# Value projections of 20 of the 64 attention units made ahead, during the gates and mixing stages

## What is computed

```python
q = query @ W_Query + B_Query          # query: normalized x after layer 0
k = key @ W_Key + B_Key                # key = value = the context
v = value @ W_Value + B_Value
scores = jnp.einsum('bqhd,bkhd->bhqk', q, k) / D ** 0.5
probs = jax.nn.softmax(scores, axis=-1)
out = jnp.einsum('bhqk,bkhd->bqhd', probs, v)
```

## Time and profile before

| | |
|---|---|
| median of 3 runs | 1844.22 us (1844.12 to 1845.14) |
| span of the profiled execution | 1843.2 us |
| busy: PE, PEld, DVE, ACT, POOL | 1663.1, 1128.1, 1209.8, 843.8, 608.1 us |
| gates stage | about 4 to 64 us of the span |
| mix and MLP | about 64 to 437 us, of it steps -2 and -1 to 126.5 us |
| attention | about 437 to 1650 us |
| one attention unit | 18.17 us |

### The profile page before, as it was taken

One profiled execution on the slowest core, in us unless ns is written; L12 is line 12 of the kernel. 1 busy time (PEld: TensorE's weight loads), 2 busy tenths in 40 slices (PEclk: granted clock), 3 DMA queues, 4 the chain that ended last, 5 costly groups with the idle time before them and its releaser, 6 DMA issues. The chain is left out here.

```text
span 1843.2 us, 25796 instructions
## 1 busy us (share of the span) xinstructions
PE 1663.1 (90%) x8789; PEld 1128.1 (61%) x8789; DVE 1209.8 (66%) x2689; ACT 843.8 (46%) x1870; POOL 608.1 (33%) x730
## 2 busy tenths in 40 slices
PE   6569999996999999999999999999999999973584
PEld 4447777754666666666666666666666766642352
DVE  6445656532777777776776776776777677757761
ACT  3324343431555555555555555555555555531110
POOL 2143445430333323332332332333232323220375
PEclk9669999997999999999999999999999999985697
DMA  8100000003323232323232322222223223213254
GB/s 254 27 23 12 12 12 1 1 0 106 69 47 69 47 92 46 69 69 69 47 92 47 67 72 61 54 65 74 56 60 79 59 53 86 46 45 99 44 85 58
DMA packets 68961, 109.46 MB, mean 59 GB/s; under 512 B 18400, under 2 KB 50400, under 8 KB 68832
## 3 DMA queue, kind: packets, MB, share of 16 engines
q1 hardware_dynamic: 62688, 99.29, 22.1%
q0 software_dynamic: 6144, 8.52, 3.0%
HBM read 27.84 MB, written 12.85 MB: 22 GB/s over the span
## 5 line engine op out<-in xcount | busy, mean ns | idle before, releaser
L1128 POOL TENSOR_SCALAR at_Pr<-at_Pr,at_rinv 128x512 f32<-128x512 f32 x512 | 355.8, 695 | 841.2 <-DVE at_rinv L1158 841.2
L1093 ACT ACTIVATE at_Pr<-at_ps,at_nmax 128x512 f32<-128x512 f32 x512 | 352.2, 688 | 535.2 <-DVE at_nmax L1153 533.6
L1153 DVE TENSOR_REDUCE at_nmax<-at_ps 128x1 f32<-128x512 f32 x512 | 351.2, 686 | 154.0 <-PE at_ps L958 142.5
L958 PE MATMUL at_ps<-at_k,at_q 128*128 128x512 f32 x1024 | 420.7, 492 | 10.8 <-DMA at_k<-at_k_own 9.1
L969 PE MATMUL at_ps<-k_ident,at_Pr 128*128 128x128 f32 x2048 | 309.8, 274 | 4.5 <-POOL at_Pr L1128 4.5
L969 PEld LDWEIGHTS at_ps<-k_ident,at_Pr 128*128 128x128 f32 x2048 | 250.5, 140 | 90.2 <-POOL at_Pr L1128 27.7
L1165 DVE COPY at_PT<-at_ps 128x512 f32<-128x512 f32 x384 | 261.4, 681 | 0.0
L958 PEld LDWEIGHTS at_ps<-at_k,at_q 128*128 128x128 f32 x1024 | 174.6, 191 | 130.7 <-issue 121.2
L979 PE MATMUL at_ps<-at_PT,at_V 128*64 128x512 f32 x1024 | 235.4, 602 | 0.9 <-DVE at_PT L1165 0.9
L1158 DVE RECIPROCAL at_rinv<-at_rsum 128x1 f32<-128x1 f32 x512 | 83.3, 163 | 161.1 <-ACT at_Pr L1093 159.1
L979 PEld LDWEIGHTS at_ps<-at_PT,at_V 128*64 128x64 f32 x1024 | 68.1, 137 | 122.5 <-issue 121.4
(11 more groups left out here) (236 smaller groups left out, 1996.5 us busy)
## 6 DMA issues: line engine op xcount, KB each, us to landing
at_k<-at_k_own SPq DMA_DIRECT2D x256, 256.0 KB, 4.3
k_x<-in_x SPq DMA_DIRECT2D x8, 512.0 KB, 8.5
mg_ctx<-in_ctx SPq DMA_DIRECT2D x8, 512.0 KB, 8.7
mx_ctxn<-in_ctx SPq DMA_DIRECT2D x8, 512.0 KB, 3.8
rows<-m_ctxT SPq DMA_DIRECT2D x16, 256.0 KB, 2.6
out<-k_x SPq DMA_DIRECT2D x8, 512.0 KB, 3.5
r_w<-in_L_ffn_w SPq DMA_DIRECT2D x16, 256.0 KB, 5.5
mx_w<-in_L_ffn_w SPq DMA_DIRECT2D x2, 1024.0 KB, 10.0
```

The costliest lines, as they stand in the source:

```text
L958: ins = pe.matmul(ps[:, S_BANK + j % 2, :], q2[:, u % 2, h, q:q + P], k2[:, u % 2, h, part, :], start=part == 0, stop=part == 1)
L1093: act.activation(Pr[:, j % 4, :], ps[:, S_BANK + j % 2, :], ACT.Exp, bias=nmax[:, j % 4:j % 4 + 1], accum_out=rsum[:, j % 4:j % 4 + 1]).th ...
L1128: pool.tensor_scalar(Pr[:, n % 4, :], Pr[:, n % 4, :], rinv[:, n % 4:n % 4 + 1], 1.0, ALU.mult, ALU.mult).then_inc(s["pn"], 1)
L1153: dve.tensor_reduce(nmax[:, j % 4:j % 4 + 1], ps[:, S_BANK + j % 2, :], AX.X, ALU.max, negate=True).then_inc(s["nmax"], 1)
```

## The change

20 of the 64 value projections (units 0 to 19) are made earlier, into two spare PSUM banks, copied by ACT into four slots of the tile `hT` (idle until step 0), written to a DRAM tensor of 20 x 256 KB by SP, and in the attention stage loaded back, one DMA per unit. The work is cut in halves of a unit (8 passes of 128 columns). 8 halves go behind the last gate map, 2 behind the first small transposes, 9 into step -2 and 21 into step -1 of the mixing, at the points named in `EARLY_HALVES`. W_Value is loaded for it into the other half of `hT`, and to make room the context's buffer in the gates stage shrinks from 8 batches to 3, so that SP waits for transposes before it loads further. `pick_half` is made in the gates stage, ahead of its wait for the gate maps.

In the attention loop the units whose successor has its values ready (u = 0 to 18) have no value projection; the key projection stands in block 0, and the query projection in block 4, where the values were. ACT takes the queries out in block 5 and DVE makes their second parts in block 5.

```diff
+EARLY_V = 20
+V_SLOTS = 4
+EARLY_HALVES = {"gates": 8, "rows": 2, (-2, "scores"): 1, (-2, "keys"): 2, (-2, "values"): 3, (-2, "states"): 3,
+                (-1, "scores"): 1, (-1, "keys"): 7, (-1, "values"): 9, (-1, "states"): 3, (-1, "turned"): 1}
+EARLY_AT = dict(zip(EARLY_HALVES, itertools.accumulate(EARLY_HALVES.values(), initial=0)))
...
+def early_values_pe(pe, fl, ctxT_all, ps, banks, point):
+
+    at = EARLY_AT[point]
+    for n, half in (divmod(h, 2) for h in range(at, at + EARLY_HALVES[point])):
+        b, hp = n // HP, n % HP
+        if half == 0 and n >= 2:
+            pe.wait_ge(fl["out"], n - 1)
+        if n == 0 and half == 0:
+            pe.wait_ge(fl["w"], 16)
+        for t in (2 * half, 2 * half + 1):
+            for d in range(DC):
+                ins = pe.matmul(ps[:, banks[n % 2], P * t:P * t + P],
+                                ctxT_all[:, d, b * S + P * t:b * S + P * t + P], fl["wv"][:, d, P * hp:P * hp + P],
+                                start=d == 0, stop=d == DC - 1)
+        if half:
+            ins.then_inc(fl["ps"], 1)
+
+
+def early_units(point):
+
+    at = EARLY_AT[point]
+    return range(at // 2, (at + EARLY_HALVES[point]) // 2)
+
+
+def early_values_act(act, fl, ps, banks, point):
+
+    for n in early_units(point):
+        act.wait_ge(fl["ps"], n + 1)
+        if n >= V_SLOTS:
+            act.wait_ge(fl[f"put{n % V_SLOTS}"], 16 * (n // V_SLOTS))
+        act.copy(fl["stage"][:, n % V_SLOTS, :], ps[:, banks[n % 2], :]).then_inc(fl["out"], 1)
+
+
+def early_values_sp(sp, fl, point):
+
+    for n in early_units(point):
+        sp.wait_ge(fl["out"], n + 1)
+        sp.dma_start(fl["dram"][n], fl["stage"][:, n % V_SLOTS, :]).then_inc(fl[f"put{n % V_SLOTS}"], 16)
...
-                    sp.dma_start(ctx_s[:, i, :, :], cv[i]).then_inc(s[f"c{i % RING}"], 16)
+                    if i >= CTX_RING:
+                        sp.wait_ge(s["ctx_turned"], i - CTX_RING + 1)
+                    sp.dma_start(ctx_s[:, i % CTX_RING, :, :], cv[i]).then_inc(s[f"c{i % RING}"], 16)
...
+                load_wv(sp)
...
+                early_values_sp(sp, fl, "gates")
+                early_values_sp(sp, fl, "rows")
...
                 gate_maps(B // 2 - 1)
+                early_values_pe(pe, fl, ctxT_all, ps, V_BANKS, "gates")
 
                 pe.wait_ge(s["rows"], 4)
                 for t in range(TPB):
                     at = R * (KIND_G + t)
                     pe.transpose(ps[:, COL_BANK, at:at + R], gg[:, P * t:P * t + P], ident[0:R, 0:R])
+                early_values_pe(pe, fl, ctxT_all, ps, V_BANKS, "rows")
...
                 act.activation(lfg[:, :], efg[:, :], ACT.Ln, bias=1.0).then_inc(s["act_rows"], 1)
+                early_values_act(act, fl, ps, V_BANKS, "gates")
                 act.wait_ge(s["rows"], 6)
...
                 act.activation(floor[:, :], logmax[:, :], ACT.Exp, scale=-1.0).then_inc(s["act_rows"], 3)
+                early_values_act(act, fl, ps, V_BANKS, "rows")
...
+                for k in range(2):
+                    at = slice(R * k, R * k + R)
+                    dve.tensor_copy(g["pick_half"][at, :, :], ident[at, at].rearrange("k (r a) -> k r a", a=1
+                                                                                   ).broadcast_to([R, R, MD]))
                 dve.wait_ge(s["fg"], 1)
...
+                    if m == 2:
+                        for point in EARLY_HALVES:
+                            if point not in ("gates", "rows"):
+                                early_values_sp(sp, fl, point)
...
                     if t == 0 and half == 0:
+                        pe.wait_ge(fl["out"], EARLY_V)
...
                         scores(m, 0)
+                        fill(b, "scores")
...
                         spread_max(m, 1)
+                        fill(b, "keys")
                         states(m, 0)
...
                         spread_max(m, 2)
+                        fill(b, "values")
                         values(m, 0)
...
-                pe.wait_ge(s["own"], 5)
...
+                    if b == 0:
+                        for k in range(V_SLOTS):
+                            act.wait_ge(fl[f"put{k}"], 16 * len(range(k, EARLY_V, V_SLOTS)))
...
                         decay(m, 0)
+                        keep_early(b, "scores")
                         decay(m, 1)
+                        keep_early(b, "keys")
+                        keep_early(b, "values")
                         decay(m, 2)
...
+                    if ready(u):
+                        if u >= 2:
+                            sp.wait_ge(s["pv"], u - 1)
+                        sp.dma_start(V[:, u % 2, :, :].rearrange("p t d -> p (t d)"), v_dram[u]
+                                     ).then_inc(s[f"v{u % 2}"], 16)
...
+                        if ready(u - 1):
+                            pe.wait_ge(s["ql"], u)
...
-                    pe.wait_ge(s["V"], u + 1)
+                    if ready(u):
+                        pe.wait_ge(s[f"v{u % 2}"], 16 * (u // 2 + 1))
+                    else:
+                        pe.wait_ge(s["V"], u - EARLY_V + 1)
...
-                        if j < 2 and there(u + 1):
+                        if j < 2 and there(u + 1) and not ready(u + 1):
                             project(u + 1, j)
+                        if j in (0, 4) and ready(u + 1):
+                            project(u + 1, 1 - j // 4)
                         if j == 2 and there(u - 1):
                             weigh_values(u - 1)
-                        if j == 4 and there(u + 1):
+                        if j == 4 and there(u + 1) and not ready(u + 1):
...
-                            if j == 0:
+                            if j == (5 if ready(u + 1) else 0):
                                 queries(u + 1)
                             if j == 1:
                                 keys(u + 1)
-                            if j == 5:
+                            if j == 5 and not ready(u + 1):
                                 values(u + 1)
...
-                            if j == 1:
+                            if j == (5 if ready(u + 1) else 1):
                                 queries(u + 1)
```

More of the change, by code:

```diff
@@ L390, in mix_and_mlp @@
         tmp_in, tmp_out = norm_tmp(sb, 2)
[L391 to L392 removed]
+        w1_s, w2_s, b1_s, b2_s, after_s, w_row, ctxn, hT = (
+            early[n] for n in "w1 w2 b1 b2 after w_row ctxn hT".split())
+        pick_half = g["pick_half"]
         vsum = sb("vsum", [P, 2, HT], F32)
@@ L816, in _, with attention @@
                     dve.memset(own[MD * h:MD * h + MD, h, :], MD ** -0.5).then_inc(s["own"], 1)
[L817 to L822 removed]
+                dve.wait_ge(s["own"], 3)
                 for b in STEPS:
                     step(b)
[L827 removed]
+def attention(nc, c, x_all, xnT_all, ctxT_all, first, Wq, Wk, Wv, Wo, gate_w, lg, rows, rows_in, out, landed,
+              v_dram):
     U = HP * B
@@ L1084, in _ @@
                 keys(0)
-                values(0)
                 for u in range(U + 1):
@@ L1659, in _, with build @@
                         read(e + AHEAD)
-def build(nc, a, rows, out):
+def build(nc, a, rows, out, v_dram):
     with ExitStack() as ctx:
@@ L1736 @@
     out = nc.dram_tensor("out_0", (N + SPARE, D), F32, kind="ExternalOutput").ap()
-    build(nc, aps, rows, out)
+    v_dram = nc.dram_tensor("v_early", (EARLY_V, P, TPB * P), F32, kind="Internal").ap()
+    build(nc, aps, rows, out, v_dram)
     r = run(nc, [arrays], core_ids=[0])
```

60 lines of the change are left out of this document (35 added, 25 removed).

## The result

| | before | after |
|---|---|---|
| median of the runs taken together, us | 1844.68 (4 runs) | 1885.61 (4 runs, 1884.09 to 1886.86) |
| ratio, 95% interval | | 1.0221 [1.0208, 1.0233] |
| span of the profiled execution, us | 1843.2 | 1882.7 |
| first score of attention unit 0 | 455.66 | 444.57 |
| first score of attention unit 20 | 821.96 | 862.09 |

The account below looks back on a forecast made before the run. Attention seemed PE-bound, but with 0.43 us of slack to the score, maximum, exponential chain. Attention +41 and front -7 gave +34 on the 1843.2 span, so 1877, and 1878 us as median; range 1852 to 1897.

Parts of the forecast that it names:

- End of a unit: Attention blocks 5 to 7: DVE's late queries delay reciprocal, maximum and exponential, so the next unit's first score comes 2.40 us later.
- Start of a unit: Attention, first score to transpose 0: without the key projection in block 1, 0.46 us is won, bounds 0 and 0.76.
- Units 1 to 18 with routing: Attention: 1.94 us more per unit, +34.9; waiting key projections in units 12 and 13, +4.1; late norm pieces, +1.5.
- Unit 0: First attention unit: no previous unit's work in the way, chain and shorter PE work about cancel; +0.5, between -2 and +2.
- Loads: Attention: the 20 value loads of 256 KB cost nothing; if late, 2.6 us would be added per unit.
- The front: Stages ahead of attention: six pieces, from gates to context ring, sum to about -7 us, between -12 and +12.
- The gates stage's end: Behind the last gate map: value halves and copies delay table load and exponentials, +1.1, or +4 if the clock fell; taken +2.
- The fills with the clock: Mixing steps -2 and -1: higher clock -9.2, halves ending late and ACT copies +2.3, first of step -2 still slow +1.5.
- The rule on matmul busy time: Attention: a full matmul row doesn't prove PE the bound, LDWEIGHTS share is 11.98 of 18.17; removed time need not return.
- PE's time comes back: Rival, attention: PE is the bound throughout and late queries do no harm; 31 us saved, 1806 us in all; 11%.
- The milder tail: Rival, attention: unit ends late by less, start gains its full 0.76; some 0.9 us per unit, 1857 us; 12%.
- the cold fills: Rival, mixing steps -2 and -1: value halves run at the lower clock; front +12, 1897 us; 12%.

Follow-up runs that it names:

- experiment 3: Changed kernel, with four passes of unread matmuls filling PE's gap at the end of units that neither turn rows nor map gates: 1877.54 us, ratio 1.0177.
- experiment 2: Changed kernel, with DVE's part of the queries one block later (block 6), ACT's part and PE's projections still late: 1848.73 us, ratio 1.0018.
- experiment 1: Changed kernel, with query and key projections and the query copies back in blocks 0 and 1, value projection still away: 1823.08 us, ratio 0.9879.
- experiment 11: Changed kernel, with the key projection back in block 1 of PE and the query projection left in block 4: 1878.66 us, ratio 1.0181.
- experiment 4: Changed kernel, with only the first two of the 20 value loads issued, so units 2 to 19 weigh old values: 1885.74 us.
- experiment 6: Changed front without early values, their copies or stores, and the attention stage of the kernel before: 1842.32 us, ratio 0.9984.
- experiment 5: Changed front with the attention stage of the kernel before; the 20 early units of values are computed and not used: 1834.80 us, ratio 0.9939.
- experiment 9: Kernel with the queries put back, with PE's output products of the unit before ahead of transposes 3 and 4: 1830.06 us, ratio 0.9921.
- experiment 10: Kernel of experiment 9, with DVE's row maximum ahead of the reciprocal in block 6 alone: 1825.02 us, ratio 0.9893.

## Why the prediction was right, point by point

The forecast was 1878, the runs gave 1885.6, inside the range of 1852 to 1897 and on the forecast side. The mechanism, late queries that hold up the end of a unit, is shown. That the sum came this close is in part luck: the loss in the attention stage was set 10 us too small (41 forecast, 51.2 measured) and the gain of the front 4 us too small (7 forecast, 11.1 measured), and the two errors went against each other. The 1.0 us that the forecast put around the span is 1.7 in every run of the record (1884.42 against 1882.7 in the profiled one).

- **End of a unit**, +2.40 forecast, +2.43 in the changed kernel and +2.37 with the clock up (experiment 3). Moved by one block, DVE's queries give back 36.9 us (experiment 2), and with all queries back the stage is faster than before (experiment 1).
- **Start of a unit**, -0.46 forecast, -0.13 measured. The working was right for a clock that stays up: experiment 3 has -0.52. The step that failed is that the first 4 us were costed at the upper level. The prediction named the delay of transpose 5 and did not ask what the clock does when PE stands idle once in each unit (1.93 us). The cost is 0.45 us per unit by experiment 3, and about 8 us over units 1 to 18 by that figure.
- **Units 1 to 18 with routing**, +40.5 forecast (34.9 + 4.1 + 1.5), +48.1 measured. At +2.28 for each ordinary unit 41.0 is the common part, and 7.1 is left for the routing units against the 5.6 forecast. Of these the key projection's place accounts for 5.8 (experiment 11), where 4.1 stood. Units 9, 10, 17 and 18, for which 1.5 stood, are 1.3 above the common part together.
- **Unit 0**, +0.5 forecast, +1.69 measured; experiment 11 takes 1.34 of it away, so it is the keys' place again, which I had costed at nothing there. **Unit 19**, not in the sum: +1.39, since it starts behind a late unit 18; filling PE's gap takes 1.0 of it away (experiment 3), so mostly the clock.
- **Loads**, nothing forecast, and experiment 4 shows nothing.
- **The front**, -7 forecast, -11.1 measured. `pick_half` -3.4 forecast, -3.2 (experiment 6). The gates stage's end +2 forecast, +0.9 measured at the exponentials (61.51 against 60.61). The fills with the clock, -9.2 + 2.3 + 1.5 = -5.4 forecast; from the first spread of step -2 to the one of step 0 it is 66.9 us (132.39 - 65.47) in place of 74.7 (143.27 - 68.59), so -7.8. So 3.1 of the 11.1 us are won up to the first spread, 7.8 from there to step 0 and 0.2 behind. The stretch of values, forecast to fall from 4.71 to 2.40 us, is at 2.42 in step -2. The clock is 0.83 between 60 and 70 us and 1.00 from there to the end of step -1, so little of the low start that I had set at 1.5 us is there.
- **The rule on matmul busy time.** By the full matmul row 1.71 us per unit were to be won; 0.60 came back with the queries in their old place (experiments 1 and 5). Transpose 3 then waits for POOL, but that wait is not the bound: without it the unit stays at 17.57 us (experiment 9). The chain of reciprocal, maximum and exponential is: with its order changed in one block, the unit falls to 17.18 (experiment 10). The Trainium skill (Perfetto Trace Analysis, Identifying the Most-Contended Engine) says that matmul busy time is no good measure of how close TensorE is to its limit. This case agrees: the row, busy for all 18.17 us, didn't show that a third of the projection is all that comes back.
- **The rivals.** *PE's time comes back* fell twice: with late queries there is a loss, and without them only a third returns. The milder tail fell with +2.43 at the end of a unit, the cold fills with a clock of 0.97.

The fastest version that was run is that of experiment 1, at 0.9879 of before: the early values kept, the queries left where they were. That of experiment 10 is the same within the intervals.

## What to carry to other kernels

Work taken off a full engine is worth what the next chain leaves of it, and an operation moved into the hole is paid for in the queues of the engines that finish it: count for each of them what stands behind it and who waits for that. Two engines that hand a value back and forth (here reciprocal, maximum, exponential at 1.60 us a block) set the end of a unit here, though neither is full. And a new idle time on TensorE has a second price, which is read from the granted clock of the stretch behind it.
